# A fused tower on one core: cross attention with all four units' logits issued together, four weight slots, and a new split of the layer norms

## The reference

```python
h = _L0_tok_ref(x, ...)                        # the top 16 of each 128 tokens are kept
h = h + _L0_attn_ref(_layernorm(h), ...)       # retention
h = h + _L0_ffn_ref(_layernorm(h), ...)        # 8 experts, top 1
h = h + _L1_attn_ref(_layernorm(h), ...)       # cross attention over videos
h = h + _L1_ffn_ref(_layernorm(h), ...)        # 8 experts, top 2

def _L1_attn_ref(text_embeds, video_embeds, Wq, bq, Wk, bk, Wv, bv, Wo, bo):
    ...
    logits = jnp.einsum('avhd,bthd->abhvt', k, q) / math.sqrt(HEAD_DIM)
    weights = jax.nn.softmax(logits, axis=3)   # over the 64 frames of one video
    attn = jnp.einsum('avhd,abhvt->abhtd', v, weights)
    attn = attn.reshape(num_vids, num_texts, num_words, EMBED)
    attn = attn.mean(axis=0)                   # over 128 videos
    return attn @ Wo.T + bo
```

## Time and profile before

| | |
|---|---|
| median of 3 runs | 2425.41 us (2425.32 to 2430.37) |
| the profiled execution | 2424.38 us, span 2422.3 us |
| busy in the span | PE 2112.0 (87%), DVE 2004.9 (83%), POOL 1762.8 (73%), ACT 1674.1 us (69%) |
| cross attention's loop | first maximum (L1842) starts at 559.0 us, last one at 2102.8 us |
| crossnorm block | 514.3 to 549.0 us |
| route blocks | 352.1 to 405.4 us, and 2128.8 to 2200.5 us |
| from the last scatter's issue | 2392.9 us to the end, 2422.3 us |

### The profile page before, as it was taken

How to read it: one execution, slowest core, us unless ns; L and a number is a source line. 1 busy time by engine, 2 the same in 40 slices (tenths; PEclk the granted TensorE clock), 3 DMA queues, 4 the chain that set the end, 5 groups by cost and what they waited for, 6 DMA issues and landing times. The chain is left out here.

```text
span 2422.3 us, 50062 instructions
## 1 busy us (share of the span) xinstructions
PE 2112.0 (87%) x14341; PEld 1631.3 (67%) x14341; DVE 2004.9 (83%) x3388; ACT 1674.1 (69%) x4826; POOL 1762.8 (73%) x1672
## 2 busy tenths in 40 slices
PE   4555876838999999999999999999999999967993
PEld 2345766835777777777777777777777777657883
DVE  6977765147999999999999999999999999776664
ACT  2153211526888888888888888888888988704662
POOL 3643432755888888888888888888888888824773
PEclk9676665968999999999999999999999999957997
DMA  7421113622222222222222222222222222143555
GB/s 247 143 70 44 35 50 90 169 70 61 66 65 66 66 65 65 66 65 65 66 65 65 66 65 65 66 66 65 66 66 65 65 66 65 44 97 107 156 156 153
DMA packets 157684, 197.68 MB, mean 82 GB/s; under 512 B 33200, under 2 KB 99888, under 8 KB 155504
## 3 DMA queue, kind: packets, MB, share of 16 engines
q1 hardware_dynamic: 139280, 174.80, 26.6%
q0 software_dynamic: 8064, 16.60, 2.5%
q10 hardware_dynamic: 10208, 4.66, 0.7%
HBM read 77.58 MB, written 17.74 MB: 39 GB/s over the span
## 5 line engine op out<-in xcount | busy, mean ns | idle before, releaser
L1958 POOL TENSOR_TENSOR attend_weights<-attend_weights,attend_scales 128x512 f32<-128x512 f32 x1024 | 1047.1, 1044 | 198.4 <-DVE attend_scales L1868 198.4
L1842 DVE TENSOR_REDUCE attend_maxima<-attend_psL 128x16 fp32r<-128x1024 f32 x512 | 618.5, 1208 | 4.7 <-PE attend_psL L1757 2.7
L1915 ACT ACTIVATE attend_turned<-attend_psT 128x512 f32<-128x512 f32 x1024 | 554.0, 595 | 36.2 <-PE attend_psT L1776 12.9
L1776 PE MATMUL attend_psT<-consts,attend_weights 128*128 128x128 f32 x4096 | 553.9, 275 | 4.6 <-POOL attend_weights L1958 2.0
L1776 PEld LDWEIGHTS attend_psT<-consts,attend_weights 128*128 128x128 f32 x4096 | 474.0, 140 | 97.3 <-POOL attend_weights L1958 14.2
L1790 PE MATMUL attend_psA<-attend_turned,attend_value_ring 128*64 128x256 f32 x4096 | 498.5, 386 | 0.8 <-ACT attend_turned L1915 0.8
L1756 PE MATMUL attend_psL<-attend_key_ring,attend_q_high 128*128 128x512 f32 x1024 | 457.7, 447 | 3.9 <-ACT attend_weights L1908 2.3
L1908 ACT ACTIVATE attend_weights<-attend_psL,attend_maxima 128x64 f32<-128x64 f32 x2048 | 449.7, 354 | 4.7 <-DVE attend_maxima L1842 4.7
L1903 ACT ACTIVATE attend_weights<-attend_weights 128x512 f32<-128x512 f32 x512 | 342.3, 669 | 135.6 <-DVE attend_weights L1852 135.6
L1757 PE MATMUL attend_psL<-attend_key_ring,attend_q_low 128*128 128x512 f32 x1024 | 403.4, 394 | 0.0
L1852 DVE TENSOR_TENSOR attend_weights<-attend_psL,attend_maxima 128x512 f32<-128x512 f32 x512 | 354.2, 692 | 52.7 <-DVE attend_maxima L1842 2.0
(11 more groups left out here) (318 smaller groups left out, 2473.6 us busy)
## 6 DMA issues: line engine op xcount, KB each, us to landing
attend_key_ring<-keys SPq DMA_DIRECT2D x512, 128.0 KB, 2.2
attend_value_ring<-values SPq DMA_DIRECT2D x128, 256.0 KB, 2.5
moe2mix_w_tile<-in_L_ffn_w_dram SPq DMA_DIRECT2D x71, 256.0 KB
select_xbuf<-in_x_dram SPq DMA_DIRECT2D x16, 1024.0 KB, 5.5
moe1mix_w_tile<-in_L_ffn_W_dram SPq DMA_DIRECT2D x39, 256.0 KB
select_emb<-L_attn_video_embeds_dram ACTq DMA_DIRECT2D x16, 256.0 KB, 4.2
values_gates<-project_vg SPq DMA_DIRECT2D x8, 512.0 KB, 2.6
retain_vg<-values_gates SPq DMA_DIRECT2D x8, 512.0 KB
```

Source lines behind the costliest of these rows:

```text
L1776: mm = pe.matmul(psT[:, j % 2, k * P:(k + 1) * P], weights[:, 4 * parity + j, k * P:(k + 1) * P], ident, is_transpose=True, start=(k == 0) ...
L1842: dve.tensor_reduce(maxima[:, both, :].rearrange("p j v -> p (j v)"), psL[:, both, :].rearrange("p j (v f) -> p (j v) f", f=FR), X, ALU.ma ...
L1915: act.activation(turned[:, parity, :, h, t, :], psT[:, j % 2, :].rearrange("p (k q) -> p k q", k=SUB), ACT.Copy).then_inc(turned_copied, 1)
L1958: pool.tensor_tensor(w, w, scales[:, s, :, None].to_broadcast([P, VC, FR]), ALU.mult).then_inc(normalised, 1)
```

## The change

Several things change together.

1. In the loop PE issues shift (of the step before), then all eight logits matmuls, then M in two halves, each followed by the T of one pair. There are four weight slots instead of two, `halves` has two places. Two of the slots are `lower` (16 KB a partition), two are `upper`, the memory of `K.hidden`, whose rows are written to DRAM (`hidden_dram`) in the crossnorm block and read back into `lower` at the end. DVE takes both maxima first and then the sums of the step before; POOL normalises step n-2 instead of n-1 in step n; ACT's order follows.
2. `LayerNorm.statistics` and `.apply` take the place of `batches` in crossnorm and in both route blocks: DVE keeps the statistics and a `shift` column, ACT writes the normalised rows. In crossnorm the addition of the experts' result moves from POOL to DVE.
3. The tables in DRAM are laid out `(p g)`: the piece of one partition in a DMA is contiguous (2 KB for a batch, 4 KB for a quarter).
4. `add_back` moves into the experts' last block: SP waits for the scatters itself.

```diff
@@ LayerNorm
+    def statistics(self, dve, hidden, before=None):
+        for b in range(B + 2):
+            if b < B:
+                if before:
+                    before(b)
+                for g in range(b * TB, (b + 1) * TB):
+                    dve.bn_stats(self.stats[:, g, :], hidden[:, g, :]).then_inc(self.steps, 1)
+            if b > 1:
+                part = slice((b - 2) * TB, (b - 1) * TB)
+                dve.wait_ge(self.root_ready, b - 1)
+                dve.scalar_tensor_tensor(self.shift[:, part], self.mv[:, part, 0], -1.0, self.root[:, part], ALU.mult, ALU.mult).then_inc(self.shift_ready, 1)
+            if b < B:
...
+                    dve.bn_aggr(self.mv[:, g, :], self.stats[:, g, :]).then_inc(self.steps, 1)
...
+                dve.tensor_scalar(self.square[:, part], self.mv[:, part, 1], self.scale, self.eps, ALU.mult, ALU.add).then_inc(self.square_ready, 1)
+    def apply(self, act, hidden, rows, ready, b):
+        act.wait_ge(self.shift_ready, b + 1)
+        for g in range(b * TB, (b + 1) * TB):
+            ins = act.activation(rows[:, g, 0:D], hidden[:, g, :], ACT.Identity, bias=self.shift[:, g:g + 1], scale=self.root[:, g:g + 1])
+        ins.then_inc(ready, 1)
@@ route_and_mix
-                    table = K.normed_dram[top].rearrange("(g p) d -> p g d", p=P)
+                    table = K.normed_dram[top].rearrange("(p g) d -> p g d", p=P)
...
+                        for n in range(RING):
+                            sp.wait_ge(result_out[n], 16 * len(range(n, used, RING)))
...
+                                sp.dma_start(back[:, k, part, :], tokens[:, part, :]).then_inc(back_in[q], 16)
@@ cross_attention, crossnorm block
+                    for b in range(B):
+                        sp.wait_ge(rows_added, b + 1)
+                        sp.dma_start(kept[:, b, :], upper[:, b, :]).then_inc(hidden_kept, 16)
...
+                    norm.statistics(dve, K.hidden, added)
@@ cross_attention, loop, SP
+                    sp.wait_ge(turned_ready, (B * STEPS - 2) * UNITS)
+                    for b in range(B):
+                        sp.dma_start(lower[:, b, :], kept[:, b, :]).then_inc(hidden_back, 16)
@@ loop, PE
+                        if exists(n - 1):
+                            shift(n - 1, 1)
...
                             logits(n, p, k, 0)
-                        if exists(n - 1):
-                            shift(n - 1, 1)
-                        if exists(n - 2):
-                            turn_weights(n - 2, k % 2, 0)
-                        if exists(n - LAG):
-                            before = quarter(i, p, q4 - 1) if k < LAG else q
-                            mix(n - LAG, before, (k - LAG) % 4, run, early == LAG)
-                        if exists(n):
-                            shift(n, 0)
                             logits(n, p, k, 1)
-                        if exists(n - 2):
-                            turn_weights(n - 2, k % 2, 1)
+                        for half in range(2):
+                            if exists(n - LAG):
+                                mix(n - LAG, before, (k - LAG) % 4, run, early == LAG, half)
+                            if exists(n - 2):
+                                turn_weights(n - 2, (k - 2) % SLOTS, half)
@@ loop, DVE
+                            if isinstance(n, int) and n == 2:
+                                dve.wait_ge(hidden_kept, B * 16)
+                            for pair in range(2):
+                                maximum(n, pair)
+                                subtract(n, k, pair, exists(n - SLOTS))
...
                         if exists(n - 1):
-                            total(n - 1, 1 - parity, 0)
-                            total(n - 1, 1 - parity, 1)
-                            invert(n - 1, 1 - parity)
-                        if exists(n):
-                            maximum(n, 1)
-                            subtract(n, parity, 1, exists(n - 2))
+                            total(n - 1, (k - 1) % SLOTS, 0)
+                            total(n - 1, (k - 1) % SLOTS, 1)
+                            invert(n - 1, (k - 1) % SLOTS)
@@ loop, POOL
-                        if exists(n - 1):
-                            normalise(n - 1, 1 - k % 2, 0)
-                        if exists(n):
-                            halve(n, k % 2)
-                        if exists(n - 1):
-                            normalise(n - 1, 1 - k % 2, 1)
+                        if exists(n - 2):
+                            normalise(n - 2, (k - 2) % SLOTS)
+                        if exists(n):
+                            halve(n, k)
```

More of the change, by code:

```diff
@@ L1227, in _ @@
                     steps.mark(dve.memset(all_ones[:], 1.0))
-                    norm.batches(dve, K.hidden, normed, norm_ready)
+                    norm.statistics(dve, K.hidden)
                     dve.wait_ge(router_in, 16 if last else 32)
@@ L1474, in _ @@
                 def _(dve):
-                    steps, later = Steps(dve, mix_steps), Steps(dve, finish_steps)
+                    steps = Steps(dve, mix_steps)
                     def of_expert(table, e):
@@ L1641, in _ @@
                     act.nop().then_inc(normT_copied, 2)
-                    with act.Fori(0, B // 2) as it:
-                        for s in range(2):
-                            b = it * 2 + s
-                            act.wait_ge(normT_ready, b + 1)
-                            act.activation(qT[:, ds(b * L, L)], psT[:, s, :], ACT.Copy).then_inc(normT_copied, 1)
+                    norm.apply(act, K.hidden, rows, norm_ready, 0)
+                    for b in range(B):
+                        if b + 1 < B:
+                            norm.apply(act, K.hidden, rows, norm_ready, b + 1)
+                        act.wait_ge(normT_ready, b + 1)
+                        act.activation(qT[:, b * L:(b + 1) * L], psT[:, b % 2, :], ACT.Copy).then_inc(normT_copied, 1)
         with ExitStack() as inner:
@@ L1893, in high, with exponentials @@
                         act.activation(q_high[p][h][:], psQ[:], ACT.Identity, bias=K.bq2[:, h:h + 1]).then_inc(q_highs, 1)
-                    def exponentials(n, parity, pair):
-                        for j in (2 * pair, 2 * pair + 1):
-                            into = weights[:, 4 * parity + j, :]
+                    def exponentials(n, slot, units):
+                        for j in units:
+                            pair = j // 2
+                            into = weights_of(slot)[:, j, :]
                             if SHIFTED_BY[j] == "TensorE":
@@ L1909, in exponentials, with copy_turned @@
                                 ins.then_inc(exped, 1)
[L1911 to L1912 removed]
+                    def copy_turned(n, parity, units):
+                        for j in units:
                             h, t = unit(j)
```

218 lines of the change are left out of this document (116 added, 102 removed).

## The result

The changed kernel takes **2458.7 us** (median of 4 runs, 2457.48 to 2460.84), the kernel before, beside it on the same chip, 2426.98 (4 runs, 2425.32 to 2430.37). The ratio is 1.013, with a 95% interval of 1.0112 to 1.0147: **slower by 32 us**. I had said slower, 2438, and the time lies inside my range, but the loss is more than twice the forecast one.

A forecast was written before the change was run, and what follows sets the result against it. DVE bounds the loop at 5.99 us a step, PE close behind; the change makes PE the bound. Loop +28, crossnorm -10, route blocks -1, end -4 sum to +13 us: 2438 us, 8-in-10 range 2416 to 2462.

The forecast's parts named there:

- Switches, 0.59 us a step: Loop, PE: entering or leaving the 64-column mix matmuls four times costs 0.14 + 3 x 0.15 = 0.59 us, against 0.34 before.
- Step of PE, 6.13: Loop: 5.54 us of work plus 0.59 of switches makes PE's step 6.13 us, above DVE's 5.99.
- four matmuls that project q at 0.22: Loop, per run: 32 x 6.13 plus these matmuls makes 197.0 us against 193.3, eight times: +30 us, taken as +28.
- DVE waits 0.1 to 0.2 us in most steps: Loop: DVE's maxima would idle for PE's logits in most steps, where they waited for nothing before.
- cover of the way back: Loop's end: reading rows back from DRAM has 12.2 us for 5.1 of issues and about 5 of landing, so costs nothing.
- Crossnorm, -10: Block ahead of the loop: 2.1 us a batch on DVE, 1.7 on ACT; ends at 538.9 instead of 549.0.
- Route blocks, -1 for both: PE's 0.20 us wait a batch goes, saving 1.4 us; first batch normalised about 1 us later; -1 us for both blocks.
- Rival C: Route blocks: PE's clock rises to 2.4 GHz, together some 14 us less, 2424 us; chance 0.08.
- End, -4: SP waits for the landing itself, 2 to 3 us less; contiguous 4 KB reads may save 0 to 3 us.
- Rival A: Loop: switches cost less than DVE's lead, the step stays 5.99 us, kernel faster at 2410 us; chance 0.17.
- Rival B: Loop: the two-step round trip through POOL becomes the bound, step 6.20 us, 2456 us; chance 0.13.

The follow-up runs named there:

- experiment 3: Kernel before, its mix matmuls split in halves around the second pair's logits, so one more entry and exit of the 64-column kind: 2482.0 us, ratio 1.0227.
- experiment 7: Changed kernel with the projection of q and ACT's high and DVE's low part of q cut to 64 of 512 columns: ratio 1.0072.
- Experiment 2: Changed kernel with the projection of q inside the loop cut to 64 of 512 columns: 2447.8 us, ratio 1.0096.
- experiment 11: Kernel before with only the new DRAM order and the merged end added; loop and LayerNorms as before: the two give 7.5 us together.
- experiment 10: Changed kernel with the loop as before and the old DRAM order, beside the same with the new order: the order's part is 5.0 us by medians.
- experiments 9 and 11: First: changed kernel with the loop as before, rerun. Second: kernel before with only new DRAM order and merged end, 7.5 us gained; LayerNorms give 12.1.
- experiments 5 to 8: POOL's normalisation halved, mix whole (1.0057) or in changed order (1.0114); changed kernel, q work cut (1.0072); changed kernel, loop as before, old DRAM order (0.9952).
- experiments 8 and 10: Changed kernel with the loop and the DRAM order as before, run on two chips: ratio 0.9952 on the slower; 5.0 us for the order on the other.

## Why the prediction was right in direction and wrong in size

By its steps, with the trace or the run that answers:

- **Switches, 0.59 us a step: right.** In the row of the profile after, T to M 0.15, M to T 0.15 twice, L to M 0.14. The one that was in no row, taken as 0.15 between 0 and 0.20, was also had apart: two switches in experiment 3 cost 0.33.
- **Step of PE, 6.13: 0.03 too low, the second term that was mis-sized.** It is 6.16. The eight logits matmuls take 1.86 by ends and not 2 x 0.92; the rest is rounding. Times 256 that is 8 us. The prediction knew that the third digit was missing and still took the low end, 28 in place of 30: 2 us more.
- **"four matmuls that project q at 0.22": the step that failed.** It put 0.9 us a run beside 32 steps. A run takes 199.4, and 199.4 - 32 x 6.16 = 2.3; the missing 1.4 us are 11 us in eight runs. Of the 1.4, 0.8 is the price of the matmul: a projection takes 0.86, not twice 0.22, and steps 1 and 3 are 0.87 and 0.83 longer than 6.16. The other 0.6 is a cost that the prediction didn't have at all: steps 2 and 4, with no projection in them, take 6.48 each, and experiment 7 takes that away by shortening the work of ACT and DVE on q, though 0.2 comes back in step 3. Experiment 2 took away 1.3 of the 2.3 us, experiment 7 another 0.4. It was in my own numbers: eight written-out steps of the kernel before last 49.5 us, and 49.5 - 8 x 5.88 = 2.5. I priced the steps that contain a projection by one that contains none, and didn't set the sum against the run that I had measured. The excess of these steps is nearly the same before (2.5) and after (2.3), so the change hardly touched it. The run of 193.3 us that I subtracted held it whole, and the run of 197.0 that I built held 0.9 of it: the difference came out too small by the rest.
- **Together**, the loop: 28 + 2 + 8 + 11 = 49, as the trace has it. Or, from the steps: 192 x (6.16 - 5.99) + 64 x (6.16 - 5.88) - 8 x 0.2 = 49.
- **DVE waits 0.1 to 0.2 us in most steps: right** (0.15), and the slots, the rows in DRAM and their way back cost nothing that a row shows: the way back is issued at 2147.12, POOL's addition starts at 2162.05 after the blocks' meeting, with no wait for it. The cover of the way back was 12.2 us in the forecast and is 14.9. No run has the four slots alone; PE's 0.6 us of idle time in 1000 us bounds what they can cost PE by waits in the loop.
- **Crossnorm, -10: it gave 8.** A batch takes 2.0 us on both engines: DVE's additions follow each other after 1.99 us, and on ACT, which comes last, copy follows copy after 2.01:

```profile
537.29 0.59 ACT L1681 ACTIVATE cross_normT<-crossnorm_psT 128x512 f32<-128x512 f32 x1
...
537.77 1.65 ACT L243 ACTIVATE crossnorm_rows<-hidden,crossnorm_shift,crossnorm_root 128x128 f32<-128x128 f32 x4
539.30 0.59 ACT L1681 ACTIVATE cross_normT<-crossnorm_psT 128x512 f32<-128x512 f32 x1
```

  DVE's pace was forecast well (2.1). ACT's was not: four activations are 1.65 us (taken as 1.1), and with the copy ACT needs 2.01 instead of 1.7. The last copy ends 23.8 us after the start of the first addition, where I said 21 to 22. `shift` of a batch stands two batches late, so ACT starts late and, being no faster than DVE, makes none of it up; that this is the whole of the 2 us is not shown.
- **Route blocks, -1 for both: it was some 2.** On PE a batch's transposes followed each other after 372.48 - 369.75 = 2.73 us before and do so after 2.45 now. The idle time of 0.20 that the earlier trace rows show ahead of the load was not all of it. But the first transposes come 5.7 us after the block's start (353.6) instead of 4.0 (352.1), which takes most of that back. From the block's start to the first gather of the next one it is 53.5 instead of 54.6 us in the first block, and 71.8 instead of 73.0 in the second. The "some 4 more" that I expected before experiment 11 was read from the pace alone. Rival C is out: PEclk in that window is still 0.50, the 1.2 GHz level. Before, and then now:

```profile
356.11 1.12 PE L1183 MATMUL moe1route_psT<-consts,moe1route_normed 128*128 128x128 f32 x4 [6.30 <-DVE moe1route_normed L236]
...
369.75 1.12 PE L1183 MATMUL moe1route_psT<-consts,moe1route_normed 128*128 128x128 f32 x4
...
372.48 1.11 PE L1183 MATMUL moe1route_psT<-consts,moe1route_normed 128*128 128x128 f32 x4
```

```profile
359.32 1.12 PE L1210 MATMUL moe1route_psT<-consts,moe1route_normed 128*128 128x128 f32 x4 [8.21 <-ACT moe1route_normed L243]
...
365.79 1.09 PE L1210 MATMUL moe1route_psT<-consts,moe1route_normed 128*128 128x128 f32 x4
...
368.24 1.09 PE L1210 MATMUL moe1route_psT<-consts,moe1route_normed 128*128 128x128 f32 x4
...
352.00:380.00 28.00, 20.17 (x96) 19.67 (x96) 11.32 (x82) 16.83 (x40) 8.79 (x9) 0.50 0.59 171
```

- **End, -4: it gave 6.7 by the traces, 7.5 by the medians.** The last scatter is issued at 2436.09 and SP reads from 2438.47, 2.4 us later in place of 6.5; that is 4, where I said 2 to 3. The reads issue in 3.92 instead of 11.11 us, which I had bounded by 3 and which gave 3 (experiment 10).

```profile
2436.09 0.97 POOL L1416 DMA_INDIRECT result<-moe2mix_result,moe_target  x1 [0.30 <-DMA result<-moe2mix_result,moe_target]
```

```profile
2438.47 3.92 SPq L1399 DMA_DIRECT2D moe2mix_back<-result  x8
```

- **Rival A** was decided by experiment 3 and the row of the step. **Rival B** is not what happened, but it was closer than its 0.13 sounds: it binds as soon as T moves ahead of M. Its price of 2456 us lies next to the measured 2458.7 by accident.

The loop's 49 us of the trace, less the 12.1 and 7.5 that the runs gave, make +29, against +32 measured (27 to 36 by the interval of the ratio). Against the forecast the loop was 21 us dearer and the rest 5 us better, so part of the loop's miss is hidden in the total. Of the 12.1 us the traces of experiments 9 and 11 place 8 in crossnorm, 1.7 in the route blocks and 1.2 in the loop, whose program is the same in both; the rest is not shown. Open stay the step 3 of experiment 7, and a few single steps of 6.4 to 7.6 us in four runs of the profiled execution, together some 2 us; and which instructions of ACT lengthen steps 2 and 4.

## What to carry to other kernels

Before pricing a new order of an in-order engine, count how often it changes the kind of its work, and price each change by ends: here they were 0.25 us a step more, enough to take the bound from DVE to PE and, over 256 steps and less the 0.11 us that PE had to spare in 192 of them, 43 of 49 us. A piece of work put between two others may be there to hide a third engine: making the mix whole saved two switches and cost 90 us, since T then met POOL's unfinished units. Set a sum of single prices against a whole stretch that the trace has, a run with its uncommon steps, before using it for the changed kernel: the excess of 2.5 us a run was in view. And measure a bundled change in parts: all but the loop was good, and without the loop it is 0.8% faster than the kernel before.

## What the runs showed of the hardware

A full fp32 matmul of 128 x 512 costs PE 0.86 us, an fp32r one of the same shape 0.23: T ends at 1161.06, the shift behind the projection at 1162.14, 1.08 later, of which the shift is 0.22.

```profile
1159.97 1.09 PE L1813 MATMUL attend_psT<-consts,hidden 128*128 128x128 f32 x8
1160.90 1.02 PE L1785 MATMUL attend_psQ<-cross_normT,wq 128*128 128x512 f32 x2
1161.36 0.78 PE L1803 MATMUL attend_psL<-attend_maxima,cross_ident_r 128*128 128x512 f32 x1
```

The two records of 0.51 us don't show it; their ends are modelled and the next row's start hides the rest. The Trainium skill, page "FP8 and Floating Point Precision", section "TensorE Precision Notes", says that true fp32 takes four passes through the array; 0.86 against 0.23 agrees (3.7 times).

POOL's multiplication took 615 ns for 256 columns and 1043 for 512. If the rest grows with the columns, about 0.19 us of each doesn't shrink with them.

On the chip of experiments 5 to 8 the loop kept its 5.98 us a step (1539.3 us from first to last step, as elsewhere), while the kernel before took 2494.3 us instead of 2426. The kernel of experiments 8 and 10, which was run on both chips, shows where the time goes: the two blocks of experts, which gather their rows from DRAM, take 132.0 and 248.7 us (the second from its first gather to the first store) on the one and 108.0 and 205.2 on the other, and the granted clock there is 0.85 and 0.87 against 0.91 and 0.93. Which of the two, the gathers or the clock, comes first is not shown. The stages between and behind them agree within 2 us; the stretch ahead of the first route block is 5 us shorter on the slower chip.
